# A decoder layer on one core: values of the cross attention scaled by GpSimd, in seven pipeline stages instead of eight

## The chip, the cores and the metric

The kernel runs on 1 core of one Trainium2 chip. The core has five engines that run side by side, each through its own list of instructions in order: TensorE (PE, its weight loads shown as PEld), VectorE (DVE), ScalarE (ACT), GpSimd (POOL) and SyncE (SP), which here only issues DMA transfers. They wait for each other through semaphores. The metric is the device time of one execution in microseconds (us); less is better.

## The reference, cut to what matters

One decoder layer: self attention with an ALiBi bias, cross attention over a context, and a quantised feed-forward part, each with a residual and a layer norm. 32 batches, 112 queries, 375 context rows, width 256, 16 heads of 16.

```python
x: (32, 112, 256)    ctx: (32, 375, 256)    all float32

def self_attention(x):
    Q, K, V = (x @ W + b for W, b in ...)              # 16 heads of 16
    attn = softmax(Q K^T / 4 + alibi, axis=keys)
    return (attn V) @ Wo + bo

def cross_attention(x, ctx):
    q = x @ Wq + bq;  k = ctx @ Wk + bk;  v = ctx @ Wv + bv
    sm = einsum('nlhd,nshd->nlhs', q, k) / 4
    sm = softmax(sm, axis=1)                           # over the QUERIES l, not over the keys s
    return einsum('nlhs,nshd->nlhd', sm, v) @ Wo + bo

x = layernorm(x + self_attention(x))
x = layernorm(x + cross_attention(x, ctx))
x = layernorm(x + ffn(x))                              # 256 -> 768 -> 256, quantised
```

The softmax of the cross attention runs over the queries. So each pair of a context row s and a head h has one divisor, and it can be put on the values: `v[s, h, :] / Z[s, h]`. This product of 125 x 128 numbers is the operation that the change moves.

## The kernel before, in words

The program has three parts: a short preparation of weights, the attention of all 32 batches (about 38 to 875 us), and the feed-forward part. The change touches only the attention.

**Units.** The cross attention of a batch is worked through in six units u = 0 to 5 (`NU`): a half t of the heads (8 heads) and a third c of the context (125 rows). A unit goes through these steps, each on one engine:
- `cross_scores` (PE, L1137): scores of 8 heads into one of two PSUM slots (`score`, a slot also serves the two halves S0 and S1 of the self attention)
- `max_cross` (DVE, L846): the largest score of each row and head
- for u = 0, 2, 3, 5: `shift` (PE, L1148) subtracts it in PSUM, `exp_shifted` (ACT, L669) makes the exponentials `Px` in one instruction, `halve_cross` (POOL, L577) adds the two halves of the queries to `Ph`, `sum_cross` (DVE, L818) sums them to `Zc`
- for u = 1, 4: `exp_by_head` (ACT, L661), eight exponentials with their own sums
- `reciprocal_cross` (DVE, L825): `rZc` = 1 / `Zc`
- `normalise_values` (DVE, L832): `Vn` = `Vx` times `rZc`, both inputs in SBUF
- `cross_values` (PE, L1160): `Vn` times `Px` into `outX`

`Px`, `Zc`, `rZc` and `Vn` have three buffers each, by u modulo 3.

**Other work of a batch.** x is transposed (`transpose_x`, PE L1079) and projected to keys and queries (`Ks`, `Qs`, `project_T`, PE L1099). Both are split into a high and a low part (`hi_...` on ACT, `lo_with_bias` on DVE L862), written to DRAM by `save_...` and read back in another layout by `lay_...` (SP). Then come `self_scores` (PE L1126), `max_self` (DVE L853), `exp_self` (ACT L650), `reciprocal_self` (DVE L890), `normalise_probs` (POOL L584: `Ps` times `rZs`, 112 x 896, also two inputs in SBUF), four `transpose_probs` (PE L1195, "PT0" to "PT3"), `self_values` (PE L1204), `project_out_self`, `residual`, `moments`, `mean_variance`, `add_eps` (DVE), `inverse_root` (POOL L591), `norm_self` (DVE L933: `x1` from `r1` and `rstd`, both in SBUF). The context is transposed (L1171), projected in three products to `Kx` (`keys_cross`) and `Vx` (`values_cross`, L1071 to L1073), drained by `hi_keys_cross` (ACT), `lo_keys_cross` (DVE L875) and `values_with_bias` (DVE L883). The last steps of a batch are `project_out_cross`, a residual, `norm_cross` (DVE L941, as `norm_self`) and `transpose_x2`.

**What sets the order.** It is written out by hand in one function `step` for each engine. A batch passes through `STAGES` steps. In step i the names n0, n1, ... are the batches i, i+1, ... up to n7, so n7 is the batch that enters and n0 the one that leaves. The steps run from `FIRST` = 1 - `STAGES` to 31; where a batch does not exist its work is left out. So there are 39 steps before: 7 in which the pipeline fills, 25 with all eight stages, and 7 in which it drains. Steps 2 to 23 are a loop, two steps in one turn.

**Banks.** Three PSUM banks `work0` to `work2` take turns by the table `WORK_USES`: of each bank it lists the uses in their order, each with the stage of its batch. A use may be filled by PE only when the one before it in the list is drained. For instance `fill` of "PT1" waits until the use ahead of it in its bank is drained. `SLOT_USES` does the same for the two slots of scores.

Of the kernel before, what the change touches and what calls it, by code (L numbers as in the profile page):

```python
# [70 lines left out]
STAGES = 8  # L71
# [10 lines left out]
)  # L82
SLOT_USES = (
    (("C5", 2), ("S1", 6), ("C1", 3), ("C3", 3)),
    (("S0", 6), ("C0", 3), ("C2", 3), ("C4", 3)),
# [241 lines left out]
def attention(nc, a, ident, x2T_all, xmax_all, x2_dram, stacks_dram, constants):  # L327
    with ExitStack() as ctx:
# [119 lines left out]
        def _(sp):  # L448
# [84 lines left out]
            def step(n0, n1, n2, n3, n4, n5, n6, n7):  # L533
                if n7:
                    load_x(n7)
                if n6:
                    lay_queries_self(n6)
                if n0:
                    save_x2(n0)
                if n3:  # L540
                    lay_keys_cross(n3, 0)
                    lay_queries_cross(n3)
                    save_keys_cross(n3, 1)
                if n6:
                    load_ctx(n6)
                if n3:
                    lay_keys_cross(n3, 1)
                if n7:
                    save_keys_self(n7)
                if n4:  # L550
                    save_keys_cross(n4, 0)
                if n7:
                    save_queries_self(n7)
                    lay_keys_self(n7)
                if n4:
                    save_queries_cross(n4)
# [4 lines left out]
        def _(pool):  # L561
# [43 lines left out]
            def step(n0, n1, n2, n3, n4, n5, n6, n7):  # L605
                if n2:
                    halve_cross(n2, 3)
                    halve_cross(n2, 5)
                if n3:
                    add_output_bias_2(n3)  # L610
                if n4:
                    inverse_root(n4, 0)
                if n6:
                    normalise_probs(n6, 0)
                    normalise_probs(n6, 1)
                if n3:
# [10 lines left out]
        def _(act):  # L627
# [115 lines left out]
            def step(n0, n1, n2, n3, n4, n5, n6, n7):  # L743
                if n5:
                    copy_probs(n5, 0)
                if n4:
                    hi_context(n4, 0)
                    hi_context(n4, 1)
                if n2:
                    exp_by_head(n2, 4)  # L750
                if n5:
                    even_self(n5, 0)
                    copy_probs(n5, 2)
                if n2:
                    exp_shifted(n2, 5)
                if n7:
                    copy_xT(n7)
                if n5:
                    even_self(n5, 1)
                if n6:  # L760
                    copy_values_self(n6)
                    exp_self(n6, 0)
                if n7:
                    hi_keys_self(n7)
                if n6:
                    exp_self(n6, 1)
                if n4:
                    hi_keys_cross(n4, 0)
                    hi_keys_cross(n4, 1)
                if n7:  # L770
                    hi_queries_self(n7)
                if n3:
                    exp_shifted(n3, 0)
                if n4:
                    copy_x1T(n4)
                if n3:
                    exp_by_head(n3, 1)
                if n2:
                    even_cross(n2)
                if n3:  # L780
                    exp_shifted(n3, 2)
                if n6:
                    copy_probs(n6, 1)
                if n4:
                    hi_queries_cross(n4)
                if n6:
                    copy_probs(n6, 3)
                if n0:
                    copy_x2T(n0)
                if n3:  # L790
                    exp_shifted(n3, 3)
# [3 lines left out]
        def _(dve):  # L795
# [154 lines left out]
            def step(n0, n1, n2, n3, n4, n5, n6, n7):  # L950
                if n0:
                    norm_cross(n0)
                if n2:
                    sum_cross(n2, 2)
                if n4:
                    lo_context(n4, 0)
                    lo_context(n4, 1)
                if n1:
                    residual(n1, 1)
                if n2:  # L960
                    reciprocal_cross(n2, 2)
                    normalise_values(n2, 2)
                    max_cross(n2, 5)
                    sum_cross(n2, 3)
                    reciprocal_cross(n2, 3)
                if n5:
                    pick_self(n5, 0)
                if n2:
                    normalise_values(n2, 3)
                if n4:  # L970
                    mean_variance(n4, 0)
                if n6:
                    max_self(n6, 0)
                if n5:
                    pick_self(n5, 1)
                if n0:
                    largest(n0)
                if n6:
                    max_self(n6, 1)
# [947 lines left out]
```

## Time and profile before

| | us |
|---|---|
| median of 3 runs | 1172.6 |
| lowest and highest | 1171.67, 1175.38 |
| the profiled execution | 1172.56 |
| its span, first to last instruction | 1170.7 |

| engine | busy in the whole span | busy of 50 us at 450 to 500 us |
|---|---|---|
| PE | 1021.1 us (87%) | 47.98 |
| DVE | 986.5 us (84%) | 47.73 |
| ACT | 889.3 us (76%) | 45.21 |
| POOL | 465.3 us (40%) | 21.77 |

Busy time counts each instruction from its recorded start to its recorded end. Neighbouring instructions of an engine overlap by 0.1 us (DVE, ACT) to 0.25 us (PE), since the next begins while the one before still drains. So a sum of durations is a little more than the time in which the engine gets through them, and the time between two starts is the better measure. A wait of a PE group hides its first part in that overlap.

### The profile page before, as it was taken

To read this page: it belongs to the slowest core of one execution; us is meant where nothing else is said; L and a number is where in the kernel's file an instruction comes from. 1 tells how busy PE (TensorE), PEld (TensorE's weight loads), DVE (VectorE), ACT (ScalarE), POOL (GpSimd) and SP (SyncE) were. 2 spreads that over 40 slices of the span, in tenths; PEclk is the share of its full clock that TensorE was granted. 3 is DMA by queue.
4 is the path that set the end of the run, shared out by engine and by line. 5 is a ranking of instruction groups with operands and counts; after the bars stand their busy time and mean duration, and the time that the engine had idled before them with its cause. 6 is when DMAs were issued, how large, how long until landed. Compare 5 with 4: busy or idle time off the path is not lost. (4 is left out here: it accounts for less than half of the span.)

```text
span 1170.7 us, 28351 instructions
## 1 busy us (share of the span) xinstructions
PE 1021.1 (87%) x7826; PEld 839.7 (72%) x7826; DVE 986.5 (84%) x2175; ACT 889.3 (76%) x3030; POOL 465.3 (40%) x396
## 2 busy tenths in 40 slices
PE   1468999999999999999999999998759999897598
PEld 1346777777778777777778777776538988786598
DVE  6324998999999999999999999999754579989698
ACT  1356987998899889998899889987534579654695
POOL 0122543444434534444444443453310037587243
PEclk9879998999999999999999999999968999999799
DMA  6234766766676767776677667664500000000133
GB/s 169 60 93 139 200 166 159 191 179 181 164 189 177 185 165 183 183 184 177 171 186 178 183 163 190 172 183 115 143 12 1 1 1 0 1 1 1 48 106 98
DMA packets 138144, 149.15 MB, mean 127 GB/s; under 512 B 17282, under 2 KB 137826, under 8 KB 138088
## 3 DMA queue, kind: packets, MB, share of 16 engines
q1 hardware_dynamic: 136128, 148.04, 47.5%
q10 hardware_dynamic: 1960, 0.42, 0.4%
q8 instruction: 27, 0.44, 0.2%
q14 instruction: 29, 0.24, 0.1%
HBM read 94.47 MB, written 53.94 MB: 127 GB/s over the span
## 5 line engine op out<-in xcount | busy, mean ns | idle before, releaser
L577 POOL TENSOR_TENSOR Ph<-Px 125x448 f32<-125x448 f32 x128 | 147.1, 1149 | 295.5 <-ACT Px L669 295.5
L661 ACT ACTIVATE Px<-score,nmax_h 125x112 f32<-125x112 f32 x512 | 173.4, 377 | 35.1 <-DVE nmax_h L846 35.0
L650 ACT ACTIVATE Ps<-score,nmax_s 112x112 f32<-112x112 f32 x512 | 175.4, 415 | 0.1
L584 POOL TENSOR_TENSOR Ps<-Ps,rZs 112x896 f32<-112x896 f32 x64 | 107.8, 1703 | 92.7 <-DVE rZs L890 92.7
L846 DVE TENSOR_REDUCE nmax_c<-score 125x8 fp32r<-125x896 f32 x128 | 136.7, 1068 | 6.3 <-PE score L1137 6.2
L650 ACT ACTIVATION_READ_ACCUMULATOR Ps<-score,nmax_s 112x1 f32 x512 | 138.1, 270 | 0.0
L1137 PE MATMUL score<-QxS,KxS 96*125 96x224 f32 x768 | 134.2, 298 | 4.5 <-ACT Px L669 1.9
L669 ACT ACTIVATE Px<-score 125x896 f32<-125x896 f32 x128 | 119.9, 937 | 20.6 <-PE score L1148 13.6
L1160 PE MATMUL outX<-Px,Vn 125*32 125x224 f32 x1536 | 107.0, 367 | 15.0 <-DVE Vn L832 14.9
L1137 PEld LDWEIGHTS score<-QxS,KxS 96*125 96x125 f32 x768 | 104.1, 192 | 22.2 <-issue 13.5
L661 ACT ACTIVATION_READ_ACCUMULATOR Px<-score,nmax_h 125x1 f32 x512 | 118.4, 231 | 0.0
L832 DVE TENSOR_TENSOR Vn<-Vx,rZc 125x128 f32<-125x128 f32 x192 | 105.1, 548 | 2.2
L696 ACT ACTIVATE PsT<-work 112x448 f32<-112x448 f32 x128 | 73.0, 571 | 22.2 <-PE work L1195 22.2
L1442 POOL TENSOR_TENSOR U<-up_q 128x1344 int32<-128x1344 int32 (+1 forms) x16 | 49.5, 3097 | 91.0 <-DVE up_q L1568 91.0
L818 DVE TENSOR_REDUCE Zc<-Ph 125x8 f32<-125x448 f32 x128 | 78.0, 609 | 4.6 <-POOL Ph L577 4.6
L853 DVE TENSOR_REDUCE nmax_s<-score 112x8 f32<-112x896 f32 x64 | 69.3, 1083 | 14.9 <-PE score L1126 14.8
L1148 PE MATMUL score<-nmax_c,unit 125*125 125x448 f32 x256 | 77.6, 385 | 3.7 <-DVE nmax_c L846 3.6
L591 POOL TENSOR_TENSOR rstd<-vare,half 112x1 f32<-112x1 f32 x64 | 35.1, 548 | 114.3 <-DVE vare L927 114.3
L1655 PE MATMUL gbank<-xq_hi,w_upT_hi 128*128 128x448 f32 x192 | 72.0, 375 | 8.7 <-ACT xq_lo L1467 8.7
L1195 PE MATMUL work<-ident,Ps 112*112 112x112 f32 x512 | 72.9, 266 | 6.2 <-POOL Ps L584 5.5
L1160 PEld LDWEIGHTS outX<-Px,Vn 125*32 125x32 f32 x1536 | 38.3, 110 | 54.3 <-DVE Vn L832 37.7
L1195 PEld LDWEIGHTS work<-ident,Ps 112*112 112x112 f32 x512 | 55.5, 135 | 24.4 <-issue 11.9
(225 smaller groups left out, 3103.1 us busy)
## 6 DMA issues: line engine op xcount, KB each, us to landing
KxS<-Kx_parts SPq DMA_DIRECT2D x192, 187.5 KB, 4.0
Kx_parts<-Kx SPq DMA_DIRECT2D x64, 375.0 KB, 3.8
ctx_in<-in_ctx SPq DMA_DIRECT2D x32, 375.0 KB
KsS<-Ks_parts SPq DMA_DIRECT2D x192, 56.0 KB, 2.1
QsS<-Qs_parts SPq DMA_DIRECT2D x96, 112.0 KB, 2.5
QxS<-Qx_parts SPq DMA_DIRECT2D x192, 56.0 KB, 3.2
Ks_parts<-Ks SPq DMA_DIRECT2D x32, 224.0 KB, 5.9
Qs_parts<-Qs SPq DMA_DIRECT2D x32, 224.0 KB, 2.2
```

What stands on the lines that cost most here:

```text
L577: pool.tensor_tensor(Ph[p][:], Px[u % NPX][:, :, 0:L // 2], Px[u % NPX][:, :, L // 2:L], ALU.add)\
L584: pool.tensor_tensor(Ps[:, h, :], Ps[:, h, :], rZs[:, h].rearrange("q (h o) -> q h o", o=1).broadcast_to([L, OCT, L]), ALU.mult)\
L650: ins = act.activation(Ps[:, g, :], score[slot][0:L, h // QUAD, (h % QUAD) * L:(h % QUAD + 1) * L], ACT.Exp, bias=nmax_s[:, g:g + 1], accu ...
L661: ins = act.activation(Px[u % NPX][:, h, :], score[SLOT_OF[f"C{u}"]][0:C, h // QUAD, (h % QUAD) * L:(h % QUAD + 1) * L], ACT.Exp, bias=max ...
L669: act.activation(Px[u % NPX][:].rearrange("s (q h) l -> s q (h l)", q=2), score[SLOT_OF[f"C{u}"]][0:C, :, 0:QW], ACT.Exp).then_inc(exp_c, 1)
L818: dve.tensor_reduce(Zc[u % NPX][:], Ph[SHIFTED.index(u) % 2][:], AX.X, ALU.add).then_inc(z_c, 1)
L832: dve.tensor_tensor(Vn[u % NPX][:], Vx[n.par][:, c, P * t:P * (t + 1)].rearrange("s (h e) -> s h e", h=OCT), rZc[u % NPX][:].rearrange("s ...
L846: dve.tensor_reduce(dst, score[SLOT_OF[f"C{u}"]][0:C, :, 0:QW].rearrange("s q (h l) -> s q h l", h=QUAD), AX.X, ALU.max, negate=True).then ...
L1137: ins = pe.matmul(score[SLOT_OF[f"C{u}"]][0:C, q, at:at + 2 * L].rearrange("s (e l) -> s e l", e=2), KxS[:, HALF * t + j, c * C:(c + 1) * ...
L1148: ins = pe.matmul(score[SLOT_OF[f"C{u}"]][0:C, q, 0:QW], unit[:], maxima.rearrange("s (h o) -> s h o", o=1).broadcast_to([C, QUAD, L]), st ...
L1160: ins = pe.matmul(outX[32 * g:32 * (g + 1), t, :], Vn[u % NPX][:, 2 * g:2 * g + 2, :].rearrange("s h e -> s (h e)"), Px[u % NPX][:, 2 * g: ...
L1195: ins = pe.transpose(b[0:L, h * L:(h + 1) * L], Ps[:, QUAD * j + h, :], ident[0:L, 0:L])
```

## The change

- `normalise_values` moves from VectorE to GpSimd, with the same operands. Two waits are added on VectorE so that it does not overwrite `rZc` and `Vx` while GpSimd may still read them.
- `STAGES` is 7 instead of 8: there are 38 steps, 6 to fill, 26 with all stages, 6 to drain. The loop still has 22 steps.
- The order of all six lists (`step` of SP, POOL, ACT, DVE, PE, and the two tables of banks and slots) is another. What is computed is the same.

```diff
-STAGES = 8
+STAGES = 7
...
 WORK_USES = (
-    (("ctxT0", 4), ("Vs", 6), ("Ks", 7), ("K1", 4), ("V2", 4), ("V1", 4), ("x2T", 0)),
-    (("PT0", 5), ("Ox", 1), ("AVs0", 5), ("xT", 7), ("V0", 4), ("Os", 5), ("Qs", 7), ("Qx", 4)),
-    (("ctxT1", 4), ("PT2", 5), ("AVs1", 5), ("K0", 4), ("x1T", 4), ("PT1", 6), ("PT3", 6)),
+    (("xT", 6), ("ctxT1", 4), ("V0", 4), ("V1", 4), ("Qs", 6), ("K1", 4), ("PT0", 5), ("ctxT0", 5)),
+    (("AVs1", 4), ("Vs", 5), ("Ox", 1), ("K0", 4), ("PT1", 5), ("PT3", 5), ("PT2", 5)),
+    (("AVs0", 4), ("Os", 4), ("Ks", 6), ("x2T", 0), ("V2", 4), ("x1T", 4), ("Qx", 4)),
 )
...
@@ gpsimd
+            def normalise_values(n, u):
+
+                t, c = divmod(u, NC)
+                pool.wait_ge(rz_c, n.times(NU, u + 1))
+                wait_drain(pool, (n, f"V{c}"))
+                wait(pool, av_done, n.times(NU, u - (NPX - 1)))
+                pool.tensor_tensor(Vn[u % NPX][:], Vx[n.par][:, c, P * t:P * (t + 1)].rearrange("s (h e) -> s h e", h=OCT),
+                                  rZc[u % NPX][:].rearrange("s (h o) -> s h o", o=1).broadcast_to([C, OCT, HD]), ALU.mult)\
+                    .then_inc(vn_done, 1)
@@ vector: normalise_values is taken out, and
@@ reciprocal_cross
+                wait(dve, vn_done, n.times(NU, u - (NPX - 1)))
                 dve.reciprocal(rZc[u % NPX][:], Zc[u % NPX][:]).then_inc(rz_c, 1)
@@ values_with_bias
+                wait(dve, vn_done, n.back(2).times(NU, NC + c + 1))
@@ step of every engine, the order of the calls; two lines of POOL's
-            def step(n0, n1, n2, n3, n4, n5, n6, n7):
+            def step(n0, n1, n2, n3, n4, n5, n6):
...
```

The lines of instructions shift a little: L584 becomes L583 (`Ps`), L591 L600 (`rstd`), L577 L576 (`Ph`), L933 L942 (`norm_self`), L875 L883 (`Kx`), and the new `Vn` on POOL is L593.

**POOL, one full step.** `Ph` is `halve_cross`, `Ps` `normalise_probs`, `rstd` `inverse_root`, `Vn` `normalise_values`, `xb` and `x1b` the biases added to the residuals. Before:

```order
L577 TENSOR_TENSOR Ph<-Px 125x448 x2
L603 TENSOR_TENSOR x1b<-x,xbo 112x256
L591 TENSOR_TENSOR rstd<-vare,half 112x1
L584 TENSOR_TENSOR Ps<-Ps,rZs 112x896 x2
L577 TENSOR_TENSOR Ph<-Px 125x448
L597 TENSOR_TENSOR xb<-x_in,abo 112x256
L577 TENSOR_TENSOR Ph<-Px 125x448
L591 TENSOR_TENSOR rstd<-vare,half 112x1
```

Now (the step's first `Vn` stands ahead of these rows):

```order
L576 TENSOR_TENSOR Ph<-Px 125x448
L600 TENSOR_TENSOR rstd<-vare,half 112x1
L593 TENSOR_TENSOR Vn<-Vx,rZc 125x128
L612 TENSOR_TENSOR x1b<-x,xbo 112x256
L576 TENSOR_TENSOR Ph<-Px 125x448
L593 TENSOR_TENSOR Vn<-Vx,rZc 125x128
L606 TENSOR_TENSOR xb<-x_in,abo 112x256
L583 TENSOR_TENSOR Ps<-Ps,rZs 112x896
L593 TENSOR_TENSOR Vn<-Vx,rZc 125x128
L600 TENSOR_TENSOR rstd<-vare,half 112x1
L583 TENSOR_TENSOR Ps<-Ps,rZs 112x896
L576 TENSOR_TENSOR Ph<-Px 125x448 x2
```

The two `Ps` stood together, behind the root of `norm_self`. Now a `Vn` and that root (the second `rstd` here) stand between them, and two `Vn` close the step.

**DVE, around `norm_self` (`x1`).** Before:

```order
L862 SCALAR_TENSOR_TENSOR Ks<-work0,abk,Ks 128x112 x2
L933 SCALAR_TENSOR_TENSOR x1<-r1,mv0,rstd0 112x256
L825 RECIPROCAL rZc2<-Zc2 125x8
L913 TENSOR_TENSOR r1<-work1,xb 112x256
L890 RECIPROCAL rZs<-Zs 112x8
L846 TENSOR_REDUCE nmax_c0<-score1 125x8
```

Now:

```order
L834 TENSOR_REDUCE Zc2<-Ph1 125x8
L892 TENSOR_TENSOR Vx0<-work0,xbv 125x256
L899 RECIPROCAL rZs<-Zs 112x8
L842 RECIPROCAL rZc2<-Zc2 125x8
L854 TENSOR_REDUCE nmax_c0<-score0 125x8
L899 RECIPROCAL rZs<-Zs 112x8
L854 TENSOR_REDUCE nmax_h0<-score1 125x8
L870 SCALAR_TENSOR_TENSOR Qs<-work0,abq,Qs 128x112 x2
L942 SCALAR_TENSOR_TENSOR x1<-r1,mv0,rstd0 112x256
L883 SCALAR_TENSOR_TENSOR Kx<-work1,xbk,Kx 128x375
L892 TENSOR_TENSOR Vx0<-work2,xbv 125x256
```

`x1` stood ahead of the reciprocals `rZs` that release the two `Ps` on POOL; now it stands behind both of them, and directly behind it comes the drain of K0 (`Kx<-work1`).

**PE, the second part of a step** (`Ps` rows are `transpose_probs`, `x` is `transpose_x1`, `Px,Vn` are `cross_values`). Now, from the transposes PT1, which follow "K0" in bank `work1`:

```order
L1196 MATMUL work<-ident,Ps 112x112 x4
L1072 MATMUL work<-ctxT_hi,xWk_hi 128x376
L1073 MATMUL work<-ctxT_lo,xWk_hi 128x376
L1074 MATMUL work<-ctxT_hi,xWk_lo 128x376
L1072 MATMUL work<-ctxT_hi,xWk_hi 128x376
L1073 MATMUL work<-ctxT_lo,xWk_hi 128x376
L1074 MATMUL work<-ctxT_hi,xWk_lo 128x376
L1080 MATMUL work<-ident,x 128x112 x2
L1149 MATMUL score<-nmax_c,unit 125x448 x2
L1138 MATMUL score<-QxS,KxS 125x224 x4
L1196 MATMUL work<-ident,Ps 112x112 x4
L1100 MATMUL work<-x1T,xWq 128x112 x4
```

All four PT now stand in the step of their own scores; before, PT0 and PT2 stood in the next step.

## Rows read from the trace of the kernel before

**Rows 1.** Windows view: stretch, length, busy us of PE, PEld, DVE, ACT, POOL; clock.

```profile
450.00:500.00 50.00, 47.98 (x415) 38.82 (x414) 47.73 (x118) 45.21 (x194) 21.77 (x21) 1.00 0.70 180
```

**Rows 2.** Waits of PE at 300 to 700 us: us in total, times, longest.

```profile
PE work L1079 <- DVE Kx L875: 4.7, 17, 0.3
PE work L1099 <- DVE Qs L862: 4.7, 17, 0.3
PE outX L1160 <- DVE Vn L832: 4.1, 17, 0.2
PE work L1079 <- DVE Vx L883: 3.5, 16, 0.2
```

**Rows 3.** Timeline of PE: start, us, engine, line, what, idle before in brackets.

```profile
505.83 0.54 PE L1148 MATMUL score<-nmax_c,unit 125*125 125x448 f32 x2
506.21 0.55 PE L1195 MATMUL work<-ident,Ps 112*112 112x112 f32 x4
...
508.71 0.62 PE L1148 MATMUL score<-nmax_c,unit 125*125 125x448 f32 x2
509.56 0.38 PE L1079 MATMUL work<-ident,x 112*128 112x112 f32 x2 [0.23 <-DVE Vx L883]
```

**Rows 4.** Groups of instructions at 300 to 700 us: count, busy us, mean ns, idle before.

```profile
L577 POOL TENSOR_TENSOR Ph<-Px 125x448 f32<-125x448 f32 x67 | 77.0, 1150 | 148.1 <-ACT Px L669 148.1
L832 DVE TENSOR_TENSOR Vn<-Vx,rZc 125x128 f32<-125x128 f32 x101 | 58.8, 582 | 1.3
L584 POOL TENSOR_TENSOR Ps<-Ps,rZs 112x896 f32<-112x896 f32 x34 | 57.3, 1707 | 30.4 <-DVE rZs L890 30.4
L818 DVE TENSOR_REDUCE Zc<-Ph 125x8 f32<-125x448 f32 x67 | 40.8, 609 | 0.0
L883 DVE TENSOR_TENSOR Vx<-work,xbv 125x256 f32<-125x256 f32 x51 | 21.1, 414 | 0.8
L875 DVE SCALAR_TENSOR_TENSOR Kx<-work,xbk,Kx 128x375 fp32r<-128x375 f32 x34 | 20.3, 596 | 0.0
L591 POOL TENSOR_TENSOR rstd<-vare,half 112x1 f32<-112x1 f32 x33 | 18.1, 547 | 46.9 <-DVE vare L927 46.9
L597 POOL TENSOR_TENSOR xb<-x_in,abo 112x256 f32<-112x256 f32 x17 | 12.4, 727 | 0.0
```

**Rows 5.** Timelines of POOL and DVE at three places, as in rows 3.

```profile
499.06 3.37 POOL L584 TENSOR_TENSOR Ps<-Ps,rZs 112x896 f32<-112x896 f32 x2 [1.76 <-DVE rZs L890]
501.33 1.25 DVE L832 TENSOR_TENSOR Vn<-Vx,rZc 125x128 f32<-125x128 f32 x1
...
509.88 0.28 DVE L832 TENSOR_TENSOR Vn<-Vx,rZc 125x128 f32<-125x128 f32 x1
...
174.29 1.14 POOL L577 TENSOR_TENSOR Ph<-Px 125x448 f32<-125x448 f32 x1 [0.27 <-ACT Px L669]
174.31 1.40 DVE L941 SCALAR_TENSOR_TENSOR x<-r,mv,rstd 112x256 f32<-112x256 f32 x1
```

**Rows 6.** PE timeline of the filling pipeline: first scores of the second and third batch.

```profile
72.41 1.06 PE L1126 MATMUL score<-KsS,QsS 102*112 102x224 f32 x4 [3.09 <-DMA QsS<-Qs_parts]
...
89.75 0.65 PE L1126 MATMUL score<-KsS,QsS 102*112 102x224 f32 x4 [1.64 <-DMA QsS<-Qs_parts]
```

**Rows 7.** DVE timeline: `norm_cross`, which opens steps 2 and 24 to 28.

```profile
225.53 0.49 DVE L941 SCALAR_TENSOR_TENSOR x<-r,mv,rstd 112x256 f32<-112x256 f32 x1
...
749.23 0.47 DVE L941 SCALAR_TENSOR_TENSOR x<-r,mv,rstd 112x256 f32<-112x256 f32 x1
772.91 0.47 DVE L941 SCALAR_TENSOR_TENSOR x<-r,mv,rstd 112x256 f32<-112x256 f32 x1
795.64 0.47 DVE L941 SCALAR_TENSOR_TENSOR x<-r,mv,rstd 112x256 f32<-112x256 f32 x1
816.07 0.48 DVE L941 SCALAR_TENSOR_TENSOR x<-r,mv,rstd 112x256 f32<-112x256 f32 x1
835.78 0.47 DVE L941 SCALAR_TENSOR_TENSOR x<-r,mv,rstd 112x256 f32<-112x256 f32 x1
```

**Rows 8.** DMA issues at 300 to 700 us: count, size of each, us to landing.

```profile
Ks_parts<-Ks SPq DMA_DIRECT2D x17, 224.0 KB, 6.0
```

More of the change, by code:

```diff
@@ L78 @@
 WORK_USES = (
[3 rows of a table removed]
[3 rows of a table added]
 )
 SLOT_USES = (
-    (("C5", 2), ("S1", 6), ("C1", 3), ("C3", 3)),
-    (("S0", 6), ("C0", 3), ("C2", 3), ("C4", 3)),
+    (("S0", 5), ("C0", 3), ("C2", 3), ("C4", 3)),
+    (("C5", 2), ("S1", 5), ("C1", 3), ("C3", 3)),
 )
@@ L531, in lay_queries_cross @@
                 lay_on_diagonal(n, "Qx", QxS, PARTS_OF_Q, qx_laid)
-            def step(n0, n1, n2, n3, n4, n5, n6, n7):
-                if n7:
-                    load_x(n7)
+            def step(n0, n1, n2, n3, n4, n5, n6):
+                if n6:
+                    load_x(n6)
+                if n3:
+                    lay_keys_cross(n3, 0)
+                    save_keys_cross(n3, 1)
+                    lay_queries_cross(n3)
+                    lay_keys_cross(n3, 1)
+                if n6:
+                    save_keys_self(n6)
+                if n0:
+                    save_x2(n0)
+                if n5:
+                    load_ctx(n5)
+                if n6:
+                    save_queries_self(n6)
+                    lay_keys_self(n6)
+                if n4:
+                    save_keys_cross(n4, 0)
                 if n6:
                     lay_queries_self(n6)
[L538 to L554, printed above, removed]
                 if n4:
@@ L948, in largest, with step @@
                                   apply_absolute_value=True).then_inc(xmax_done, 1)
-            def step(n0, n1, n2, n3, n4, n5, n6, n7):
+            def step(n0, n1, n2, n3, n4, n5, n6):
+                if n0:
+                    mean_variance(n0, 1)
+                if n2:
+                    max_cross(n2, 4)
+                if n4:
+                    pick_self(n4, 0)
+                if n0:
+                    add_eps(n0, 1)
+                if n4:
+                    pick_self(n4, 1)
+                if n2:
+                    max_cross(n2, 5)
+                if n4:
+                    lo_context(n4, 0)
+                if n2:
+                    sum_cross(n2, 3)
+                if n4:
+                    residual(n4, 0)
+                if n5:
+                    max_self(n5, 0)
+                if n4:
+                    moments(n4, 0)
                 if n0:
                     norm_cross(n0)
+                if n4:
+                    lo_context(n4, 1)
                 if n2:
[L954 to L957, printed above, removed]
+                    reciprocal_cross(n2, 3)
                 if n1:
                     residual(n1, 1)
+                if n5:
+                    max_self(n5, 1)
+                if n4:
+                    values_with_bias(n4, 0)
                 if n2:
[L961 to L969, printed above, removed]
+                    reciprocal_cross(n2, 4)
                 if n4:
                     mean_variance(n4, 0)
+                if n1:
+                    moments(n1, 1)
                 if n6:
[L973 to L979, printed above, removed]
+                    lo_with_bias(n6, "Ks", Ks, bcol["abk"], ks_hi)
+                if n4:
+                    add_eps(n4, 0)
                 if n2:
@@ L1256, in step @@
                     cross_values(n2, 5)
+                if n4:
+                    values_cross(n4, 2)
                 if n3:
                     cross_scores(n3, 2)
+                if n5:
+                    transpose_probs(n5, 1)
+                if n4:
+                    keys_cross(n4, 1)
+                    transpose_x1(n4)
+                if n3:
+                    shift(n3, 2)
+                    cross_scores(n3, 3)
+                if n5:
+                    transpose_probs(n5, 3)
                 if n4:
                     project_T(n4, "Qx", w["xWq"], x1T, "x1T")
[L1261 to L1269 removed]
+                if n5:
+                    transpose_probs(n5, 0)
                 if n3:
                     cross_scores(n3, 4)
[L1272 to L1273 removed]
+                if n5:
+                    transpose_probs(n5, 2)
                 if n3:
                     shift(n3, 3)
[L1276 to L1277 removed]
+                if n5:
+                    transpose_ctx(n5, 0)
                 if n3:
                     cross_values(n3, 0)
[L1280 removed]
             iterations(pe, step)
```

231 lines of the change are left out of this document (95 added, 136 removed).

## Prediction

> **What bounds the kernel now.** I read the windows view first. In the middle of the attention the clock of PE is granted in full (1.00, the 2.4 GHz level), and in 50 us PE is busy for 47.98, DVE for 47.73, ACT for 45.21, POOL for 21.77 [rows 1]. So no single engine binds: PE and DVE are both full, and a gain on one is worth nothing unless the other follows. The unit of all that follows is the full step: norm_cross opens step 2 at 225.53 and step 24 at 749.23 [rows 7], so 22 steps take 523.7 us, 23.8 us each.
>
> The waits of PE come next. Each step holds four (17 or 16 of each in 400 us), every one for DVE: for the drain of a K, of Qs, of a V, and for Vn. Together 17.0 us in 400, 1.0 us a step [rows 2]. That is only the visible part. A shift without a wait is followed by the next group 0.38 us after its start (505.83 to 506.21); one with a wait of 0.23 us is followed after 0.85 us (508.71 to 509.56) [rows 3]. The wait is therefore worth 0.47 us, about 0.2 us more than its idle time, since the end of the shift overlaps the idle engine. Four such waits are some 1.75 us, so PE could get through a step in 23.8 - 1.75 = 22.1 us (estimate). ACT, busy for 45.21 of 50, needs about 21.3 us of a step.
>
> Why is DVE late? The timelines of DVE and POOL side by side show it. A Vn on DVE takes 0.28 us when POOL is idle (509.88). The one at 501.33 takes 1.25 us: it ends at 502.58, just after POOL's pair of Ps from 499.06 to 502.43 [rows 5]. The mean of all Vn is 582 ns [rows 4], so a step's six lose 6 x 0.3 = 1.8 us. It is not Vn alone: norm_cross at 174.31 took 1.40 us instead of 0.47, and ended at 175.71, 0.28 us behind POOL's Ph, which had begun 0.02 us ahead of it and ended at 175.43 [rows 5, 7]. Both have two inputs in SBUF; DVE's operations on PSUM show nothing of the kind in the timeline.
>
> The Trainium skill ("SBUF — State Buffer", section "SBUF: two separate sides") states this as a rule: a DVE operation with two SBUF inputs and a GpSimd operation share a port pair under an exclusive lock, and the later one blocks for the whole of the first. The trace agrees with it at 501.33 and at 174.31.
>
> **The change part by part.**
>
> *Vn leaves DVE.* Six times 0.58 us less (3.5 us a step) [rows 4]. DVE then needs about 19.3 us of a step and is no longer full; PE with 22.1 and ACT with 21.3 are next. PE's wait for Vn could come back through POOL (below).
>
> *Vn on POOL.* No row shows it. Bounds: not less than DVE's free 0.28 us [rows 5], not more than POOL's add of twice as many elements, 0.73 us [rows 4]. From 256 to 448 elements POOL's time rises by 1150 - 727 = 423 ns, 2.2 ns an element, which gives 727 - 128 x 2.2 = 0.45; from 256 to 896 (Ps) it rises by 1.53 ns an element, which gives 0.53. I take 0.5. Six of them put 3.0 us on POOL, which is busy for 10.4 us of a step: room enough as a sum. Only the place of each counts.
>
> The Trainium skill ("GPSIMD Engine Reference", section 4.1 "Engine selection") speaks against the move: elementwise work on GpSimd is about twice as slow as on VectorE. By that estimate a Vn is 0.56 us, and the time below would be 2 us more. No run so far shows the operation on POOL.
>
> *The new order.* I followed one step through all engines, with the time from start to start of each group, and looked for what each waits for. With no collision on the shared operands PE waits hardly at all (0.3 us in sum, for pick_self ahead of Os and for V0 and Vn5), ACT fits beside it, and the step would be 22.4 us. But one place collides. On POOL the order is now Ps of the first half, Vn, rstd, Ps of the second half. norm_self on DVE needs that rstd, so it can never start before POOL turns to the second Ps, whose own input (rZs) is ready by then, as DVE has done both reciprocals ahead of norm_self. Both have two SBUF inputs. By 174.31 [rows 5] norm_self then stays until that Ps ends. Before, rstd was followed by a wait of POOL for rZs (1.76 us ahead of the Ps pair at 499.06 [rows 5]), and norm_self slipped in.
>
> What is queued behind norm_self: the drain of K0, on which PE's transposes PT1 wait (same bank); then V2, the maximum of unit 2, the sum of unit 0. So the step becomes a loop that goes through this place. Its length, from the start of the first Ps:
> - POOL: Ps 1.7, Vn 0.5, rstd 0.55, Ps 1.7 [rows 4]: 4.45
> - norm_self beyond the end of Ps, until the next on DVE may start: 0.28 [rows 5] less the overlap of 0.1: 0.2
> - drain of K0: 0.6 [rows 4] and 0.05 to PE: 0.65
> - PE from PT1 to the end of the step and on through V1 of the next: the 22.1 us of a step less what stands between V1 and PT1. That is one cross_values 0.5, the transposes of x2 0.35, Qs 0.85, three cross_scores 1.5, a shift 0.4, two cross_values 0.95, V2 0.8: 5.3. So 16.8, and 0.15 for the wait for pick_self: 16.95
> - DVE behind V1: Zc 0.6, Vx 0.4, the reciprocal rZs 0.2, and 0.05 to POOL: 1.25 (the first two from [rows 4])
>
> Sum 23.5 us, against 23.8 now: 0.3 us a step. Removing DVE's load is worth 1.4 us a step, and the collision takes 1.1 of it back. There are 27 steps of that kind (-2 to 24, the nearly full ones included): 27 x 0.3 = 8 us.
>
> *One stage less.* The fill loses one step. The scores of the second and of the third batch begin 17.3 us apart (72.41, 89.75), held by transfers [rows 6]: what is skipped at the start is worth 17.3. It is paid back in part at the end, where the steps 25, 26 and 27 now carry one stage more. The steps 24 to 27 last 23.7, 22.7, 20.4 and 19.7 us [rows 7]; shifted by one, the three cost 23.7 - 19.7 = 4.0 more. Net 13.3 us.
>
> *SP's queue.* load_x, the self keys and queries go a round trip over DRAM within a step and a bit. The save of Ks takes 6.0 us to land [rows 8], issued about 11 us into the step; the nine transfers that lay keys and queries are out by 21.5 and landed about 1 us into the next step, while PE wants them 4.9 us into it, by the same hand count. That slack hides all of it; a round trip 4 us longer would put the rest on each step.
>
> Sum: 13.3 + 8 = 21 us. The profiled execution took 1172.56 us, its span is 1170.7, and it stands 0.04 us from the median 1172.6. 1172.6 - 21.3 = **1151 us**.
>
> **The rivals.**
>
> *A, no collision* (chance 0.18). norm_self is not blocked, or comes into its place at another time than my hand count says. For it: the same operation takes 0.47 us at each start in rows 7, so it is blocked only when POOL is ahead of it. Against: here POOL is always ahead, since norm_self waits for the operation that stands directly in front of the second Ps. Then the step is 22.4: 27 x 1.4 = 38, and 1172.6 - 13.3 - 38 = 1121 us.
>
> *B, the gain is only the fill, or a part of it* (0.12). The loop is about 0.4 us longer than counted, through a wait of 0.2 to 0.4 us that I have not seen, or late transfers. Steps of 23.9 to 24.1 give 1172.6 - 13.3 + 27 x 0.1 to 0.3, so 1162 to 1167; with half the gain of the fill lost too, 1170.
>
> *C, slower: POOL's Vn is dear* (0.10). Vn costs more than it does by size, through the broadcast of 16 elements a head or the dispatch on POOL. One Vn is in the loop between the Ps, and two close the step behind Ph of unit 2; the next step's first cross_values waits for the last of them and has some 0.7 us to spare. With x beyond 0.5 us for each, the step grows by 3x - 0.7 once x is over 0.25 or so. The fill's 13.3 us are used up at +0.5 us a step over now, so 3x - 0.7 = 0.8 and Vn = 1.0 us: the point from which it decides. At 1.1 us the step is 24.6, 27 x 0.8 = 22, and the time 1181 us. Against: twice the elements take 0.73 [rows 4].
>
> **How the numbers follow.** The forecast has 0.60, its own range 1140 to 1162: 0.3 us a step more or less is 8 us, and the fill may be worth 3 less. The range reaches down to A (1121) and up over B: 1119 to 1173, with 0.05 left out below and 0.13 above. A measurement of this kernel tells 0.3% (3.5 us) from no change. Faster by more than that: forecast and A, 0.78, and 0.03 of B: 0.81. Within it: 0.09 (B). Slower: 0.10 (C).
>
> **What would show it.** Right: a step of 23.5 us at mid attention; Vn on POOL at 0.45 to 0.55 us; norm_self on DVE at 1.2 to 1.9 us, ending with the second Ps; PE waiting for Kx once a step, for 0.8 us or more, ahead of PT1; the first norm_self about 15 us earlier (81 instead of 96); DVE at 80 to 85% busy. Wrong: norm_self at 0.47 us and a step near 22.4 (A); PE idle for transfers or for several small waits (B); Vn on POOL at 1 us or more, and PE waiting for it at the start of a step (C). The feed-forward part must keep its length of about 295 us; if it moves, the sum says nothing.

## The result

The changed kernel takes 1162.6 us (median of 5 runs, 1160.9 to 1169.2) against 1172.6 before (5 runs): 0.9928 of the time, 95% interval 0.9901 to 0.9956. So it is 8.4 us faster by the ratio, with an interval of 5 to 12, and 10 by the medians. Forecast were 1151 us, 21 us less. The sign was right, but the gain is less than half of what was claimed. The time lies just above the forecast's own range (1140 to 1162), where rival B stood, and inside the whole range of 1119 to 1173 only because that had been widened over B.

The profiled execution took 1161.5 us, its span is 1159.7. The windows view in the middle, in the columns of [rows 1]:

```profile
450.00:500.00 50.00, 46.37 (x436) 38.31 (x437) 44.75 (x103) 45.24 (x182) 25.32 (x34) 1.00 0.63 176
```

DVE fell from 47.73 to 44.75, 90% of the 50 us, where 80 to 85% had been named: the time in which norm_self is held counts as busy. POOL rose by 3.6. But PE, which was to become the full engine, fell from 47.98 to 46.37. The view of PE's waits at 300 to 700 us has one row where [rows 2] had four:

```profile
PE work L1196 <- DVE Kx L883: 28.9, 16, 1.8
```

It is the wait forecast, of PT1 for the drain of K0, and it is 1.8 us each time, where 0.8 or more was named. The timelines of DVE and POOL at that place show why (start, us, engine, line):

```profile
513.20 0.56 DVE L870 SCALAR_TENSOR_TENSOR Qs<-work,abq,Qs 128x112 fp32r<-128x112 f32 x2
513.68 2.31 DVE L942 SCALAR_TENSOR_TENSOR x<-r,mv,rstd 112x256 f32<-112x256 f32 x1
515.92 0.60 DVE L883 SCALAR_TENSOR_TENSOR Kx<-work,xbk,Kx 128x375 fp32r<-128x375 f32 x1
```

```profile
510.43 1.68 POOL L583 TENSOR_TENSOR Ps<-Ps,rZs 112x896 f32<-112x896 f32 x1 [0.44 <-DVE rZs L899]
512.07 0.40 POOL L593 TENSOR_TENSOR Vn<-Vx,rZc 125x128 f32<-125x128 f32 x1
512.43 0.55 POOL L600 TENSOR_TENSOR rstd<-vare,half 112x1 f32<-112x1 f32 x1
512.94 1.68 POOL L583 TENSOR_TENSOR Ps<-Ps,rZs 112x896 f32<-112x896 f32 x1
514.58 1.13 POOL L576 TENSOR_TENSOR Ph<-Px 125x448 f32<-125x448 f32 x1
```

norm_self was due at 513.68, while the second Ps ran. It ended at 515.99. That is not 0.28 us behind Ps (514.62) but 0.28 us behind the Ph that follows it (515.71): it was passed over twice. Its median over all 32 batches is 2.3 us:

```profile
L942 DVE SCALAR_TENSOR_TENSOR x<-r,mv,rstd x32: 472/2315/2957, 81.1 to 823.4; 112x256 f32<-112x256 f32 x32
```

Where the 11 us of the span came from, by marks that both traces have. The marks are the first cross scores of batches 4, 28 and 31 on PE and the first matmul of the feed-forward part. After:

```profile
195.22 0.68 PE L1138 MATMUL score<-QxS,KxS 96*125 96x224 f32 x4
...
775.76 0.68 PE L1138 MATMUL score<-QxS,KxS 96*125 96x224 f32 x4
...
837.91 1.10 PE L1138 MATMUL score<-QxS,KxS 96*125 96x224 f32 x8 [1.72 <-DMA QxS<-Qx_parts]
...
870.01 0.74 PE L1656 MATMUL gbank<-xq_hi,w_gateT_hi 128*128 128x448 f32 x1 [4.04 <-ACT xq_lo L1468]
```

and before:

```profile
212.16 0.78 PE L1137 MATMUL score<-QxS,KxS 96*125 96x224 f32 x4
...
782.64 0.79 PE L1137 MATMUL score<-QxS,KxS 96*125 96x224 f32 x4
...
843.26 1.15 PE L1137 MATMUL score<-QxS,KxS 96*125 96x224 f32 x4 [1.82 <-DMA QxS<-Qx_parts]
...
880.39 0.74 PE L1655 MATMUL gbank<-xq_hi,w_gateT_hi 128*128 128x448 f32 x1 [4.04 <-ACT xq_lo L1467]
```

| stretch | before | after | change | forecast |
|---|---|---|---|---|
| to C0 of batch 4 | 212.2 | 195.2 | -16.9 | -18.2 (17.3, and 3 of 27 steps at -0.3) |
| 24 steps, to C0 of batch 28 | 570.5 | 580.5 | +10.1 | -7.2 (24 of 27 steps at -0.3) |
| three steps, to C0 of batch 31 | 60.6 | 62.2 | +1.5 | +4.0 |
| to the feed-forward part | 37.1 | 32.1 | -5.0 | 0 |
| the rest | 290.3 | 289.7 | -0.6 | 0 |

The fill came out near its forecast. The middle is the wrong term, by 17 us, and it is even slower than before. Some 12 of the 17 us are the ordinary step, 24.04 us where 23.5 was forecast. Some 6 more are four long steps (2, 10, 22 and 23) of 25.3 to 25.7 us, each with one stretch of 3.4 us of lower clock. The first and the last of the 24, in which norm_self took 1.3 us, are 22.96 and 22.82 us long and give 1 us back. The starts of norm_cross show one of the long steps, 25.7 us between the first two rows and 24.0 between the last two:

```profile
407.71 0.47 DVE L950 SCALAR_TENSOR_TENSOR x<-r,mv,rstd 112x256 f32<-112x256 f32 x1
433.37 0.47 DVE L950 SCALAR_TENSOR_TENSOR x<-r,mv,rstd 112x256 f32<-112x256 f32 x1
457.35 0.47 DVE L950 SCALAR_TENSOR_TENSOR x<-r,mv,rstd 112x256 f32<-112x256 f32 x1
```

In the windows of 1 us of that step (busy us of PE, PEld, DVE, ACT, POOL, then the granted clock) PE is first idle, in the wait for K0, then busy again, and then the clock is 0.5 (the 1.2 GHz level) for some 3 us:

```profile
418.00:419.00 1.00, 0.15 (x2) 0.15 (x3) 1.00 (x3) 0.53 (x4) 0.00 (x0) 1.00 0.71 187
419.00:420.00 1.00, 1.00 (x9) 1.00 (x9) 1.00 (x3) 0.52 (x1) 0.00 (x0) 1.00 0.49 123
420.00:421.00 1.00, 1.00 (x6) 0.92 (x6) 0.97 (x2) 0.32 (x2) 0.00 (x0) 0.57 0.85 292
421.00:422.00 1.00, 1.00 (x5) 0.92 (x4) 0.81 (x2) 0.60 (x3) 0.00 (x0) 0.50 1.00 258
422.00:423.00 1.00, 1.00 (x7) 1.00 (x7) 0.34 (x1) 1.00 (x2) 0.00 (x1) 0.50 0.81 216
423.00:424.00 1.00, 1.00 (x8) 1.00 (x8) 1.00 (x2) 0.72 (x2) 1.00 (x1) 0.72 0.03 10
```

### The profile page after: what moved, and what is told of

Its sections match the earlier page's. It is cut to its first block and busy times, and to the rows that moved or that the text cites. A ratio compares the mean times of both kernels' runs of the same rounds, so it can differ in the third digit from the quotient of the medians.

```text
span 1159.7 us, 28563 instructions
## 1 busy us (share of the span) xinstructions
PE 1002.5 (86%) x7826; PEld 853.9 (74%) x7826; DVE 948.6 (82%) x1983; ACT 900.1 (78%) x3030; POOL 532.3 (46%) x588
## 5 line engine op out<-in xcount | busy, mean ns | idle before, releaser
L576 POOL TENSOR_TENSOR Ph<-Px 125x448 f32<-125x448 f32 x128 | 147.2, 1150 | 170.7 <-ACT Px L686 170.7
L593 POOL TENSOR_TENSOR Vn<-Vx,rZc 125x128 f32<-125x128 f32 x192 | 75.9, 402 | 182.5 <-DVE rZc L842 182.5
L1138 PE MATMUL score<-QxS,KxS 96*125 96x224 f32 x768 | 127.7, 290 | 3.9 <-DMA QxS<-Qx_parts 2.0
L667 ACT ACTIVATION_READ_ACCUMULATOR Ps<-score,nmax_s 112x1 f32 x512 | 129.5, 253 | 0.0
L583 POOL TENSOR_TENSOR Ps<-Ps,rZs 112x896 f32<-112x896 f32 x64 | 107.7, 1682 | 42.5 <-DVE rZs L899 42.4
L1196 PE MATMUL work<-ident,Ps 112*112 112x112 f32 x512 | 75.6, 273 | 57.2 <-DVE Kx L883 52.6
L678 ACT ACTIVATION_READ_ACCUMULATOR Px<-score,nmax_h 125x1 f32 x512 | 115.0, 225 | 0.0
L1161 PE MATMUL outX<-Px,Vn 125*32 125x224 f32 x1536 | 100.4, 365 | 1.9 <-POOL Vn L593 1.9
L713 ACT ACTIVATE PsT<-work 112x448 f32<-112x448 f32 x128 | 69.7, 545 | 35.6 <-PE work L1196 31.6
L1149 PE MATMUL score<-nmax_c,unit 125*125 125x448 f32 x256 | 80.8, 398 | 5.6 <-DVE nmax_c L854 5.6
L854 DVE TENSOR_REDUCE nmax_h<-score 125x8 f32<-125x896 f32 x64 | 69.0, 1079 | 11.7 <-PE score L1138 11.5
L1657 PE MATMUL gbank<-xq_lo,w_upT_hi 128*128 128x448 f32 x192 | 71.0, 370 | 0.0
```

The source lines that it names most:

```text
L576: pool.tensor_tensor(Ph[p][:], Px[u % NPX][:, :, 0:L // 2], Px[u % NPX][:, :, L // 2:L], ALU.add)\
L583: pool.tensor_tensor(Ps[:, h, :], Ps[:, h, :], rZs[:, h].rearrange("q (h o) -> q h o", o=1).broadcast_to([L, OCT, L]), ALU.mult)\
L593: pool.tensor_tensor(Vn[u % NPX][:], Vx[n.par][:, c, P * t:P * (t + 1)].rearrange("s (h e) -> s h e", h=OCT), rZc[u % NPX][:].rearrange("s ...
L667: ins = act.activation(Ps[:, g, :], score[slot][0:L, h // QUAD, (h % QUAD) * L:(h % QUAD + 1) * L], ACT.Exp, bias=nmax_s[:, g:g + 1], accu ...
L678: ins = act.activation(Px[u % NPX][:, h, :], score[SLOT_OF[f"C{u}"]][0:C, h // QUAD, (h % QUAD) * L:(h % QUAD + 1) * L], ACT.Exp, bias=max ...
L854: dve.tensor_reduce(dst, score[SLOT_OF[f"C{u}"]][0:C, :, 0:QW].rearrange("s q (h l) -> s q h l", h=QUAD), AX.X, ALU.max, negate=True).then ...
```

## The experiments

Nine runs followed. The theory (1): the price is norm_self, held behind POOL's operations, with the drain of K0 and so PE queued behind it. The rival (2): the new order is bound elsewhere, and the long norm_self fills a wait that is there anyway. The step is the mean of the 22 steps between norm_cross of batches 2 and 24, low-clock stretches included; norm_self is the median in the loop.

| run | what | norm_self, us | step, us | time, us | ratio to before, 95% |
|---|---|---|---|---|---|
| before | | 0.48 | 23.80 | 1172.6 | |
| after | | 2.3 | 24.31 | 1162.6 | 0.990 to 0.996 |
| e1 | norm_self when POOL has nothing running | 0.48 | 22.07 | 1101.3 | 0.936 to 0.941 |
| e2 | Ph ahead of the second Ps | 0.48 | 22.21 | 1112.7 | 0.944 to 0.950 |
| e3 | Vn back on DVE, new order | 0.68 | 24.80 | 1183.8 | 1.006 to 1.012 |
| e4 | Vn on POOL, old order, 8 stages | 0.48 | 22.50 | 1131.4 | 0.961 to 0.967 |
| e5 | a short memset between Ps and Ph | 2.35 | 25.05 | 1181.6 | 1.007 to 1.015 |
| e6 | norm_self behind the drains of K0, V2 | 1.30 | 23.21 | 1136.0 | 0.968 to 0.971 |
| e7 | e1 with each Vn made twice | 0.48 | 22.71 | 1121.4 | 0.956 to 0.959 |
| e8 | Ph waits for norm_self | 1.22 | 22.96 | 1128.8 | 0.958 to 0.965 |
| e9 | after, again | 2.3 | 24.24 | 1158.7 | 0.986 to 0.992 |

**e1, norm_self where nothing meets it.**

The order of the calls, without the conditions around them:

```diff
@@ POOL step
     normalise_values(n2, 4)
+    inverse_root(n4, 0)
+    normalise_values(n2, 5)
+    normalise_probs(n5, 0)
+    normalise_probs(n5, 1)
+    halve_cross(n3, 0)
     add_output_bias(n5)
-    normalise_probs(n5, 0)
-    normalise_values(n2, 5)
-    inverse_root(n4, 0)
-    normalise_probs(n5, 1)
-    halve_cross(n3, 0)
     halve_cross(n3, 2)
@@ DVE step
     values_with_bias(n4, 1)
+    norm_self(n4)
+    reciprocal_cross(n2, 5)
     reciprocal_self(n5, 0)
-    reciprocal_cross(n2, 5)
...
-    norm_self(n4)
     lo_keys_cross(n4, 0)
```

> The changed kernel, but norm_self's root (inverse_root) now stands on POOL ahead of Vn5 and both Ps, the bias add xb behind halve of unit 0, and norm_self on DVE stands ahead of the reciprocals rZs that release Ps. So POOL has nothing running when norm_self starts. Theory 1 (norm_self is held behind the second Ps and also behind the Ph that follows it, 2.3 us instead of 0.47, and PE waits 1.8 us a step for the drain of K0 behind it): norm_self back to 0.47 us, PE's wait for Kx gone, a step of 22.3 to 22.7 us, and a time of 1115 to 1130 us. Theory 2 (the order is bound elsewhere, by DVE's or ACT's chain of waits, and the long norm_self only fills a wait that is there anyway): norm_self 0.47 us but the step stays at 23.7 to 24.1 us, time 1155 to 1165 us.

Measured: 1101.3 us, the fastest kernel of the study, 6% below before. norm_self takes 0.48 us, since POOL is idle, waiting for rZc, when it starts. POOL, and DVE's row:

```profile
516.81 0.55 POOL L600 TENSOR_TENSOR rstd<-vare,half 112x1 f32<-112x1 f32 x1 [0.18 <-DVE vare L942]
518.23 0.40 POOL L593 TENSOR_TENSOR Vn<-Vx,rZc 125x128 f32<-125x128 f32 x1 [0.87 <-DVE rZc L848]
```

```profile
517.55 0.48 DVE L948 SCALAR_TENSOR_TENSOR x<-r,mv,rstd 112x256 f32<-112x256 f32 x1
```

PE has no wait left in its view at 300 to 650 us, and is busy for all of the 50 us:

```profile
450.00:500.00 50.00, 49.98 (x456) 41.44 (x455) 45.10 (x114) 48.65 (x207) 29.97 (x38) 1.00 0.65 184
```

The step is 22.07 us, which is the 22.1 that the prediction had worked out as what PE needs. Theory 2 falls. The edit shifts several calls at once; e2, e6 and e8 change one thing each and agree with it. The step is a little below what was expected, and the time is well below: C0 of batch 4 comes at 186.0 us instead of 195.2, so the fill gains as well.

**e2, one swap on POOL.**

```diff
     inverse_root(n4, 0)
+    halve_cross(n3, 0)
     normalise_probs(n5, 1)
-    halve_cross(n3, 0)
```

> The changed kernel with one edit: on POOL the halving of unit 0 (Ph) stands ahead of the second Ps, not behind it. POOL then waits for ACT's exponentials between the root and Ph, or runs Ph alone while norm_self is due. Theory 1: norm_self meets at most one operation at a time: 0.5 to 1.7 us instead of 2.3, step 22.5 to 23.4 us, time 1125 to 1148 us. Theory 2: no change beyond 3 us, 1158 to 1165 us.

Measured: 1112.7 us, 50 us off for one swapped line. In the loop POOL waits for ACT's exponentials ahead of Ph, and norm_self gets through in 0.48 us: it starts 0.05 us ahead of Ph (509.47 and 509.52), and it is Ph that is longer then, 1.44 us. In the steps before and behind the loop it meets Ph and takes 1.3 us, and there the step is 22.8 us. The time came out below my expectation for theory 1, on its side.

**e3 and e4, the parts of the change one by one.** In e3 `normalise_values` is on DVE again, each right behind its `reciprocal_cross`, and POOL's list is the new one without it.

> The new order and seven stages alone: Vn is put back on DVE, each behind its reciprocal, and POOL's list is the new one without the Vn. Theory 1: DVE carries six more operations a step of 0.28 us each and more where one meets Ps or Ph on POOL (one or two a step), and norm_self is still held; step 24.5 to 25.5 us, time 1175 to 1200 us. Theory 2 (moving Vn is worth nothing in this order, since DVE has idle time in it): 1160 to 1166 us.

In e4 the eight stages and all the old lists stay, and only the six products move. POOL's step then reads:

```diff
+    normalise_values(n2, 2)
     halve_cross(n2, 3)
+    normalise_values(n2, 3)
     halve_cross(n2, 5)
     add_output_bias_2(n3)
     inverse_root(n4, 0)
+    normalise_values(n2, 4)
+    normalise_values(n2, 5)
     normalise_probs(n6, 0)
     normalise_probs(n6, 1)
     halve_cross(n3, 0)
     add_output_bias(n6)
+    normalise_values(n3, 0)
     halve_cross(n3, 2)
+    normalise_values(n3, 1)
     inverse_root(n1, 1)
```

> The move of Vn alone: the kernel before with its eight stages and its order, and the six Vn on POOL, each at the place that its reciprocal allows. Theory 1 (DVE's lateness through collisions was what PE's four waits of a step stood for): those waits shrink, norm_self stays at 0.5 to 0.9 us, step 22.5 to 23.2 us, time 1135 to 1160 us, so better than the changed kernel although it has a stage more. Theory 2 (the old order is bound by its chain through ACT and PE, DVE's load does not matter): 1168 to 1174 us.

Measured: the new order with seven stages alone is slower than before (1183.8 us, ratio 1.009), the move alone is worth 41 us (1131.4, 4 us below the range named). So the move carried the gain, and with the order as it was written 31 of its 41 us are gone again. It is not the order as a whole that costs them: with norm_self at another place (e1) the seven stages come to 1101.3 us, 30 below e4.

In e3 the step and the time are as expected, but norm_self is not held: it takes 0.68 us in every step of the loop. What is held there is a Vn, which DVE starts 0.12 us behind the first Ps. It takes 1.72 us, and PE waits 1.4 us for the maximum queued behind it:

```profile
523.48 1.68 POOL L583 TENSOR_TENSOR Ps<-Ps,rZs 112x896 f32<-112x896 f32 x1 [1.40 <-DVE rZs L891]
523.60 1.72 DVE L832 TENSOR_TENSOR Vn<-Vx,rZc 125x128 f32<-125x128 f32 x1
525.24 1.08 DVE L846 TENSOR_REDUCE nmax_c<-score 125x8 fp32r<-125x896 f32 x1
526.37 0.64 PE L1147 MATMUL score<-nmax_c,unit 125*125 125x448 f32 x2 [1.43 <-DVE nmax_c L846]
```

So e3 is a second case of the same kind, with another operation, and it says nothing of the price of norm_self.

In e4 Vn on POOL costs no more than in the changed kernel, and PE has one wait left in its view at 300 to 650 us, 15 times, 6.5 us together. POOL's row for the products:

```profile
L594 POOL TENSOR_TENSOR Vn<-Vx,rZc 125x128 f32<-125x128 f32 x93 | 37.4, 402 | 105.2 <-DVE rZc L850 103.4
```

**e5, a pause between Ps and Ph.**

```diff
     normalise_probs(n5, 1)
+    pool.memset(gap[:], 0.0).then_inc(gap_done, 1)
     halve_cross(n3, 0)
```

> The changed kernel with one instruction more on POOL: a memset of one column (it reads nothing in SBUF) between the second Ps and the Ph that follows it. Theory 1a (norm_self is passed over a second time because POOL's next operation with SBUF inputs is ready at once; a pause lets VectorE in): norm_self 1.3 us instead of 2.3, PE's wait for Kx some 0.7 us instead of 1.8, step 22.8 to 23.3 us, time 1125 to 1145 us. That is the kernel that the prediction had reckoned with, so it also tests the other terms of its loop (23.5). Theory 1b (POOL keeps the operands as long as its queue has work, whatever it is): norm_self stays at 2.3 us or more, time 1160 to 1166 us.

Measured: a miss. norm_self stays at 2.35 us in the loop. The memset is over within 0.06 us (517.38 to the start of Ph at 517.44), and Ph still comes first:

```profile
515.76 1.69 POOL L585 TENSOR_TENSOR Ps<-Ps,rZs 112x896 f32<-112x896 f32 x1
517.38 0.10 POOL L639 MEMSET gap<- 112x1 f32 x1
517.44 1.14 POOL L578 TENSOR_TENSOR Ph<-Px 125x448 f32<-125x448 f32 x1
```

So a pause of 0.06 us is not enough. That fits theory 1b, though 1b's time was missed too; the run cannot tell a queue that must be empty from a pause that is too short. The kernel is 19 us slower than the changed one, and with it comes the clock: from step 10 on all 14 steps in the loop last about 25.6 us instead of 24.1, each with a stretch of lower clock. Why here in every step, and in the changed kernel in four, is not shown. PE's wait is 1.9 us, and the granted clock at 450 to 500 us is 0.93.

```profile
450.00:500.00 50.00, 46.30 (x389) 38.98 (x382) 42.38 (x96) 43.02 (x177) 24.47 (x33) 0.93 0.62 170
```

**e6, another queue behind the held operation.**

```diff
-    norm_self(n4)
     lo_keys_cross(n4, 0)
     values_with_bias(n4, 2)
+    norm_self(n4)
```

> The changed kernel with one edit on DVE: norm_self stands behind the drain of K0 and of V2 instead of ahead of them; it is still due while POOL runs the second Ps and Ph. If the price is the K0 drain queued behind it (theory 1): PE's wait ahead of PT1 is gone, norm_self still takes 1.2 to 2.0 us, the maximum of unit 2 and x1's transposes come late instead, step 22.4 to 23.2 us, time 1115 to 1145 us. If any place behind the blocked norm_self costs the same, since DVE loses the time anyway: 1155 to 1165 us.

Measured: 1136.0 us; the step is 23.2 us, at the upper end of what I expected. norm_self now starts 0.1 us after Ph, later than the second Ps, and waits only for that (1.3 us). PE's wait for Kx is gone; in its place PE waits for the maximum of unit 2, which is queued behind norm_self now:

```profile
PE score L1149 <- DVE nmax_c L854: 15.6, 17, 0.9
```

**e7, is POOL's list tight?** The kernel e1, and in `normalise_values` the product is first made into a spare buffer.

```diff
+    pool.tensor_tensor(Vspare[:], Vx..., rZc..., ALU.mult).then_inc(spare_done, 1)
     pool.tensor_tensor(Vn[u % NPX][:], Vx..., rZc..., ALU.mult).then_inc(vn_done, 1)
```

> The kernel with norm_self first (1101 us), with every Vn made twice on POOL, once into a spare buffer and once into Vn: 6 x 0.4 us more on POOL in a step. If POOL has room wherever a Vn stands (theory 1: PE is the bound at 22.07 us a step): at most 0.3 us a step, 1101 to 1110 us. If the loop through POOL is tight (the prediction's rival C: one Vn between, two at the step's end), the step grows by 3 x 0.4 - 0.7 = 0.5 us or more, 1113 to 1130 us.

Measured: 0.64 us more a step (22.71) and 20 us in all. POOL is busy for two thirds of the time only (95.8 us of 150), and yet 2.4 us of added work in a step show as 0.64: a longer Vn on POOL is not free, as rival C had supposed. That the size is near C's 3 x 0.4 - 0.7 = 0.5 proves little: the 0.7 was counted for the changed kernel, and in e1's order no Vn stands between the two Ps. Which wait carries the 0.64 is not shown; PE's waits in its view, for a maximum and for Vx, are 0.2 us at most. C's price, a Vn of 1 us, did not come.

**e8, the collision with Ps alone.**

```diff
     normalise_probs(n5, 1)
+    pool.wait_ge(x1_done, n4.times(1, 1))
     halve_cross(n3, 0)
```

> The changed kernel with one wait more on POOL: the Ph behind the second Ps waits until norm_self (x1_done) is through, so VectorE surely gets the operands when Ps ends. That is the collision as the prediction had it, with Ps alone. If the missing term of the forecast was the second time that norm_self is passed over (theory 1): norm_self 1.3 us in every step, PE's wait for Kx 0.5 to 0.9 us, the step 22.8 us as in the few steps of the changed kernel in which norm_self took 1.3 us, the clock at 1.00 throughout the middle, and a time of 1125 to 1140 us. If the loop is long for another reason: step above 23.6, 1150 us or more.

Measured: 1128.8 us, as expected. One more wait on POOL makes the kernel 34 us faster than the changed one.

```profile
517.95 1.23 DVE L944 SCALAR_TENSOR_TENSOR x<-r,mv,rstd 112x256 f32<-112x256 f32 x1
519.09 0.60 DVE L885 SCALAR_TENSOR_TENSOR Kx<-work,xbk,Kx 128x375 fp32r<-128x375 f32 x1
```

```profile
517.21 1.68 POOL L583 TENSOR_TENSOR Ps<-Ps,rZs 112x896 f32<-112x896 f32 x1
519.41 1.14 POOL L576 TENSOR_TENSOR Ph<-Px 125x448 f32<-125x448 f32 x1 [0.52 <-DVE x L944]
```

Ps ends at 518.89, norm_self at 519.18, and the drain of K0 starts at 519.09. PE's wait is down to 0.7 us, and the granted clock is 1.00 in all windows of the middle.

```profile
PE work L1198 <- DVE Kx L885: 11.4, 17, 0.7
```

**e9, the changed kernel again.**

> The changed kernel itself once more, unchanged, to see how its times spread and how many steps of 25.6 us (with a lower clock) another execution has. If those steps make the spread: time minus 1.6 us times their number is the same within 1 us for both profiles; 1158 to 1175 us.

Measured: 1158.7 us (1158.4 to 1162.7), in the range, but the test of the long steps missed. Its profile has three of them (steps 8, 9 and 12) against four, and its span is 3.0 us shorter; less 1.6 for the one step that leaves 1.4 us, where within 1 had been named. By the marks, the fill is 4.9 us shorter (C0 of batch 4 at 190.29 us), the 24 steps 0.4, and behind C0 of batch 31 it loses 2.1 us again (34.2 against 32.1). In the fill two things differ: norm_self took 1.3 us in steps -2 and -1, where it took 2.3 us in the first profile, and the clock was at its lower level for 6.8 us ahead of C0 of batch 4 instead of 23.9. So whether norm_self is passed over once or twice can change from one execution to the next, and so can the time of the fill.

## Where the prediction held and where it failed

- **The bound before.** Right: DVE was late through collisions with POOL, and PE needs 22.1 us of a step. e1 has 22.07, and e4 shows what Vn on DVE had cost, its time and its collisions together: 41 us with nothing changed but the engine of these products.
- **Vn on POOL.** 0.40 us; 0.5 was taken. Inside the bounds, and the slope of 2.2 ns an element (0.45) was the better guess. The Trainium skill's factor of about two over DVE ("GPSIMD Engine Reference", section 4.1 "Engine selection") would make 0.56, an estimate; the measured 0.40 against DVE's 0.28 is a factor of 1.4.
- **The collision.** Place, cause and the queue behind it were right. The step that failed is its term in the loop, "norm_self beyond the end of Ps, until the next on DVE may start", put at 0.2 us. It measured 1.3 us in the loop (Ps ends at 514.62, the next on DVE starts at 515.92), since the Ph behind Ps goes first as well: 1.1 us of a step that the sum had at nothing. The prediction had read the rule off 174.31 [rows 5], where nothing of POOL's stood ready behind the Ph. The Trainium skill ("SBUF — State Buffer", section "SBUF: two separate sides") says that whichever of the two starts first has the pair for its whole instruction. For norm_self and Ps the trace agrees. By the recorded starts norm_self (513.68) stands ahead of the Ph (514.58) as well, and yet it ended 0.28 us behind it (515.99): there the measurement decides.
- **The loop's other terms** were 0.5 us too long together, which hid half of that error by luck. From the first Ps to the second: 2.51 us (2.75 taken). From the second Ps until the next on DVE: 2.98 (1.9 taken). Drain of K0 to PE: 0.65 (0.65). From PT1 on PE round to the next first Ps: 17.9, the rest of the 24.04 (18.2 taken). With the collision as forecast, in e8, the loop is 22.96 us, not 23.5, and the time 1128.8 us. So had the collision been as forecast, the time would have come out 22 us below the 1151: the miss of 12 us is what two errors of opposite sign left, and the clock.
- **The clock.** Not in the prediction. The four long steps cost some 6 us, and come with PE waits of 1.8 us in every step. e3, with waits of up to 1.4 us, has three long steps too (26.0 to 26.5 us). The kernels whose waits of PE are 0.9 us or less (e1, e2, e4, e6, e7, e8) have none in the loop. This is a link seen in eleven profiles; what makes one step long and not its neighbour is not shown.
- **Fill and drain.** The fill gave 16.9 us against 18.2, its three steps of the middle included. The closeness is in part luck: in e9 the same kernel gave 21.9, and the lower clock ahead of C0 of batch 4 lasted 34 us before, 24 in the first profile and 7 in e9. The three steps 25 to 27 cost 1.5 instead of 4.0. norm_self is passed over once only in steps 24 and 25 (1.3 us, steps of 22.8 and 22.7), which may be why; no run tests it. The last stretch gave 5.0 us that were not counted, and 2.9 in e9. e4, with the old order and eight stages, gives 1.2 of them (35.9 us from C0 of batch 31), e1 has 32.9. So most of it comes with the new order and its seven stages; no run takes it apart further.
- **The rivals.** A's kernel exists, as e1: its step was given as 22.4 and its time as 1121; it is 22.07 and 1101. B's outcome came closest (1162 to 1167), with an ordinary step of 24.0, but not through a wait "that I have not seen": through the one that was seen, mis-sized. C did not come about.

What stays open is when VectorE gets in between two operations of POOL. In the steps written out singly it often does (norm_self 1.3 us at 176.12, with the Ph behind Ps stretched from 1.13 to 1.39 us); in the loop it never did in the changed kernel, with the same instructions in the same order, and with norm_self due equally far ahead of the end of Ps (0.95 us at 176.12, 0.94 at 513.68). In e3 norm_self stands at the same place between Qs and K0, starts 0.4 us before the end of Ps, and gets in ahead of the Ph right behind it in every step of the loop (0.68 us, with that Ph at 1.28). Before, Vn got in between Ps and Ph in 27 steps (1.25 us, [rows 5]), and was passed over once (2.34 us at 188.95).

## What to carry to other kernels

When an operation leaves VectorE for GpSimd, list what both engines run with two SBUF inputs, and find for each on VectorE what GpSimd has ready at that time. As the worst case, count all that it has ready, not only the operation in hand. Place the VectorE operation where GpSimd waits for something anyway, or let GpSimd wait for it: one wait more made this kernel 34 us faster. And price a stall by what is queued behind it: a norm_self of 1.2 to 1.3 us cost 0.9 us a step in e8 (22.96 against e1's 22.07) and 1.1 in e6 (23.21), and one of 2.3 us cost 2.2 in the changed kernel (24.31), its stretches of lower clock included. In e3 the same happened to a Vn of 1.7 us: look again at every such pair after each change of the order.

## What the runs showed of the hardware

- An operation of VectorE with two SBUF inputs (0.48 us alone) took 2.31 us beside a Ps and a Ph of GpSimd back to back, and ended 0.28 us after the second. A pause of 0.06 us between the two did not let it in; a wait of GpSimd for it did (1.22 us). In e3, where it started 0.4 us before the end of Ps, it got in between Ps and Ph without any help (0.68 us).
- GpSimd multiplies 125 x 128 elements of float32 in 0.40 us, against 0.28 us on VectorE undisturbed and 0.58 as a mean beside GpSimd's work [rows 4].
- PE waits of 1.8 to 1.9 us in each step of 24 us came with single stretches of 3.4 us at the 1.2 GHz level, which began between 0.1 us before and 1.5 us after PE had gone back to work: in 4 and in 3 of 24 steps (the two profiles of the changed kernel), and in 14 of 22 (e5). In e3, whose waits were up to 1.4 us, there were three. With waits of up to 0.9 us (e1, e2, e4, e6, e7, e8) there were none in the loop. Each such step was some 1.5 us longer.
